# A fused mLSTM and mixture-of-experts kernel: last down products, exponent operands and ranking reordered in the steady passes

## Chip, cores and metric

One core of a Trainium2 chip. The metric is the device time of one execution in microseconds, here the median of three runs. Engines are called TensorE (PE, with its weight loads PEld), VectorE (DVE), ScalarE (ACT), GpSimd (POOL) and SyncE (SP, which issues DMAs).

## What is computed

The input `x` is 8 batches of 512 tokens with 256 features, `ctx` the same shape. The first layer adds an mLSTM attention of the normed `x` against `ctx`, with 8 heads of 32; the second adds two shared experts and the best two of eight routed experts. Cut to what matters:

```python
# attention, per batch; q = layernorm(x), k = v = ctx
cs = cumsum(log_sigmoid(fg), axis=1)                   # fg, ig: gates of [q, k, v], 8 heads x 512
log_D = where(causal, cs[:, :, None] - cs[:, None, :], -inf) + ig[:, None, :]
m = max(log_D, axis=-1, keepdims=True)
C = (q @ k.T) / sqrt(32) * exp(log_D - m)
h = C / (maximum(abs(C.sum(-1)), exp(-m)) + 1e-6) @ v  # then a layernorm with ln_scale
x = x + h
# experts on u = layernorm(x), 256 -> 1024 -> 256
h_s = sum over 2 shared experts of gelu(rmsnorm(u, g_s) @ W1_s + b1_s) @ W2_s + b2_s
scores = sigmoid(u @ centroids)                        # 8 routed experts, top 2
h_r = sum over the 2 chosen of score / scores.sum() * expert(rmsnorm(u, g_r))
out = x + u + h_s + h_r
```

## The kernel before

**Two stages.** The first stage (to about 850 us) does, for each of 8 batches, the attention, the shared experts and the routing, and scatters token rows sorted by expert to DRAM. The second stage runs the routed experts on tiles of 256 sorted tokens and adds them to the output. The change touches the first stage only.

**Tiling.** A batch has J = 4 blocks of 128 tokens. Attention is chunked: within a block the full causal product, and across blocks a state. The shared experts are cut into U = 16 units (2 experts x 8 hidden chunks of 128). One unit is six up matmuls (L1091), a GELU (L569) and a cast to the high half (L572) on ScalarE, the low half by a subtraction on VectorE (L811), and 12 down matmuls (L1074, `second`), which accumulate over all 16 units in two PSUM banks. Matrices are split in high and low halves, so that three matmuls make one product. `second` of unit k runs in unit k + LAG with LAG = 2; behind the last unit stand the two that are left. Hidden chunks sit in NHB = 3 rotating buffers.

**Order of work.** `passes` (L363) walks, on every engine alike, a list of step letters; each letter calls the part of that step that the engine has. Pass b does the shared experts and the routing of batch b, the attention ("back") of batch b + 1 and the start ("front") of batch b + 2. The lists are START (before the first batch), FIRST (pass 0), ORDER (passes 1 to 5 and 7) and ORDER_6 (pass 6). Each engine runs its own instructions in the order of the letters; between engines there are semaphores only. The letters:

- `U`: one unit. `H`: `hand_over`: ScalarE casts the normed tokens to their high half (`xhs`, L608), VectorE makes the low half (`xls`, L825). The first unit of a batch needs both.
- `S` and the digits, `T`, `V`, `W`, `X`: steps of `back`. In `S` GpSimd's weighted values (`wv`, L478, in the buffer `chunk`) are multiplied into the states (TensorE L997) and masked (VectorE L735). Each block has two steps with its number. The first: TensorE computes the decay exponents (L1012, L1014, from `exp_lhs` and `exp_rhs`) and scores (L1023); ScalarE takes exp (L546); VectorE multiplies both (L743, into `chunk`). The second: TensorE does the inter-block product (L1040, blocks 1 to 3) and P·V (L1045); VectorE gathers the numerators (L751 to L759). Scores of block j wait until the numerators of block j - 1 are gathered. `T` to `X` do the norms, the transposes (L1054) and the logits (L1062, L804).
- `F`, `G`, `R`, `C`: steps of `front` (`f`, `g` for batches 0 and 1): `F` twice, layer norm statistics (L620) and the normed `qn` (L641); `G` transposes, copies (L521) and head masks (L676); `R` gates; `C` the transposed rows (L983), their columns and exponents on VectorE (L699 to L711), exp on ScalarE (L536), and the exponent operands on VectorE (L713 to L723).
- `A`, `Q`, `B`, `D`, `E`: steps of `route`: `A` exp of the logits on ScalarE (L580) and the ranking on VectorE (L835 to L846); `Q` gates and rows (L850 to L869); `B` counts; `D`, `E` the bias product. `P` is VectorE's sum of the residual terms (L830).
- `finish`, at the end of each pass: VectorE waits until all 16 `second` are done, adds the down banks to `base` (L818), ScalarE issues the output DMA (L576).

The exponent operands are a number cut in three bf16 parts: `head16` (L713), the rest (L714), `tail16` (L715), the rest of that (L716), and the third part, copied to `exp_lhs` (L717) and `low16` (L718), from which eight instructions (L723) fill `exp_rhs` and signal `lhs_ready`. The lines that set the seam between two passes, in `second` and `finish`:

```python
pe.wait_ge(hlo_ready, U * b + k + 1)        # second: low half of chunk k
dve.wait_ge(unit_done, U * b + U)           # finish, VectorE
sc.wait_ge(fin_ready, b + 1)                # finish, ScalarE, then the output DMA
pe.wait_ge(lhs_ready, b + 1)                # back, ahead of the first exponent matmul
```

Of the kernel before, what the change touches and what calls it, by code (L numbers as in the profile page):

```python
# [12 lines left out]
P = 128  # L13
# [6 lines left out]
def xattn_moe_kernel(nc, x, ctxt, ig_w, ig_b, fg_w, fg_b, ln_scale, g_s, W1_s, b1_s, W2_s, b2_s,  # L20
# [40 lines left out]
    with whole:  # L61
# [288 lines left out]
        START = "f f f w w w f f w w f S w w w 0 w w 0 w w 1 w w 1 w 2 w 2 3 3 T T T V V V W h u X u".split()  # L350
        FIRST = "g g U U g U U g U g U U U g U U S 0 U 0 A 1 U 1 Q F 2 U F 2 B P 3 U 3 D G T E T T R V V V R W X C".split()
        ORDER = "S 0 H 0 U A 1 U F 1 U Q 2 U F 2 B U P 3 U 3 D U G T E U T U Z T U Z R V U V U V U R U W U X C U".split()
        ORDER_6 = "S 0 H 0 U A 1 U 1 U Q 2 U 2 B U P 3 U 3 D U T E U T T U V U V V U W U X U U U U".split()
# [7 lines left out]
        def passes(engine, parts):  # L361

            backs, fronts, routes = {}, {}, {}  # L363
            for b in range(-1, B):
                k, w = START.count("u") if b == 0 else 0, 0
                for step in START if b < 0 else FIRST if b == 0 else ORDER_6 if b == B - 2 else ORDER:
# [11 lines left out]
                    elif step == "H":  # L378
                        parts["hand_over"](b)
                    elif step == "P":  # L380
# [7 lines left out]
                    elif step in "FGRCfg":  # L388
# [9 lines left out]
                if b >= 0:  # L398
                    parts["finish"](b)
# [14 lines left out]
        with nc.Block() as block:  # L414
# [99 lines left out]
            def _(sc):  # L514
                def front(b):
# [7 lines left out]
                    yield  # L523
                    sc.wait_ge(gates_done, b + 1)
# [11 lines left out]
                    nc.scalar.activation(eexp[:, :], earg[:, :], ACT.Exp).then_inc(eexp_ready, 1)  # L536
                    yield
# [67 lines left out]
                def hand_over(b):  # L605
# [5 lines left out]
                            "base": lambda b: None, "finish": finish, "route": route})  # L611

            @block.vector
            def _(dve):
# [47 lines left out]
                def front(b):  # L662
# [9 lines left out]
                    if b == 0:  # L672
                        gate_weights()
                    dve.wait_ge(qcT_ready, J * b + J)
# [40 lines left out]
                    own.done(nc.vector.tensor_copy(tail16, rest[:, 0, :]))  # L715
                    own.done(stt(rest[:, 1, :], tail16, take_two[:, :], rest[:, 0, :], ALU.mult, ALU.add))  # L716
# [178 lines left out]
                def tables():  # L895
# [44 lines left out]
                    for h in range(TJ):  # L940
# [6 lines left out]
                             "base": to_add, "finish": finish, "route": route})  # L947

            @block.tensor
            def _(pe):  # L950
                mm, tr = nc.tensor.matmul, nc.tensor.transpose

                def front(b):
# [17 lines left out]
                    yield  # L971
                    pe.wait_ge(qcT_ready, J * b + J)
# [9 lines left out]
                    for j in range(J):  # L982
# [3 lines left out]
                       ends_rhs[:, :, :].rearrange("p j h -> p (j h)"), start=True, stop=True).then_inc(cols_done, 1)  # L986
                    yield
# [79 lines left out]
                def second(b, k):  # L1067

                    pe.wait_ge(hlo_ready, U * b + k + 1)
                    e, m = k // M, k % M  # L1070
# [9 lines left out]
                def unit(b, k):  # L1080
# [366 lines left out]
```

## Time and profile before

| what | value |
|---|---|
| three runs, median (lowest to highest) | 1325.37 us (1324.14 to 1329.71) |
| the profiled execution | 1325.87 us, span 1324.1 us |
| TensorE busy | 1160.5 us, 88% of the span |
| VectorE busy | 941.8 us, 71% |
| ScalarE busy | 805.9 us, 61% |
| GpSimd busy | 348.4 us, 26% |
| mean granted clock of TensorE | 0.933 |
| one GELU of a chunk (L569, 128x512) | 0.69 us |
| sum of all waits, P·V (L1045) for the decay product (L743) | 24.4 us in 13 |
| sum of all waits, second products (L1074) for the low half (L811) | 27.4 us in 7 |
| sum of all waits, ScalarE at L546 for the final sum (L818) | 46.9 us in 5 |

Busy time counts instructions at work, not waits. TensorE's matmuls are pipelined: a row's duration is from its start to its modelled end, and the next may start before it. The granted clock is TensorE's: 1.00 is 2.4 GHz, 0.50 is 1.2 GHz. In a timeline row the bracket at the end gives the idle time of that engine ahead of the row and what ended it.

### The profile page before, as it was taken

To read this page: it belongs to the slowest core of one execution; us is meant where nothing else is said; L and a number is where in the kernel's file an instruction comes from. 1 tells how busy PE (TensorE), PEld (TensorE's weight loads), DVE (VectorE), ACT (ScalarE), POOL (GpSimd) and SP (SyncE) were. 2 spreads that over 40 slices of the span, in tenths; PEclk is the share of its full clock that TensorE was granted. 3 is DMA by queue.
4 is the path that set the end of the run, shared out by engine and by line. 5 is a ranking of instruction groups with operands and counts; after the bars stand their busy time and mean duration, and the time that the engine had idled before them with its cause. 6 is when DMAs were issued, how large, how long until landed. Compare 5 with 4: busy or idle time off the path is not lost. (4 is left out here: it accounts for less than half of the span.)

```text
span 1324.1 us, 21782 instructions
## 1 busy us (share of the span) xinstructions
PE 1160.5 (88%) x7861; PEld 1016.8 (77%) x7861; DVE 941.8 (71%) x2263; ACT 805.9 (61%) x1392; POOL 348.4 (26%) x319
## 2 busy tenths in 40 slices
PE   2839984898998997997997979799999999999996
PEld 1537763677676775885875867799999999999996
DVE  6765659677686686595694545488888888888883
ACT  3315532554554564453564425399999999999994
POOL 7102132041131221221320202023333333333333
PEclk8859885999998998998998989899999999999998
DMA  5000000110010010010000103578888888888882
GB/s 184 32 17 17 16 33 32 32 64 33 19 47 33 29 37 32 33 33 32 33 17 17 41 1 113 160 228 236 232 219 219 223 234 237 236 226 221 219 223 25
DMA packets 141690, 136.16 MB, mean 103 GB/s; under 512 B 48598, under 2 KB 127584, under 8 KB 141584
## 3 DMA queue, kind: packets, MB, share of 16 engines
q1 hardware_dynamic: 122948, 111.68, 26.7%
q0 software_dynamic: 14304, 18.75, 8.5%
q10 hardware_dynamic: 4332, 4.34, 0.9%
q8 instruction: 63, 1.03, 0.3%
q14 instruction: 43, 0.35, 0.1%
HBM read 109.42 MB, written 25.33 MB: 102 GB/s over the span
## 5 line engine op out<-in xcount | busy, mean ns | idle before, releaser
L1328 DVE TENSOR_TENSOR wlo<-big,whi 128x512 fp32r<-128x512 f32 x312 | 220.1, 717 | 21.5 <-ACT whi L1281 14.3
L569 ACT ACTIVATE shared_hraw<-bank,b1s 128x512 f32<-128x512 f32 x128 | 88.0, 688 | 196.4 <-PE bank L1091 196.2
L1281 ACT CAST whi<-big 128x512 fp32r<-128x512 f32 x312 | 191.1, 615 | 5.4 <-PEq L414 5.1
L1253 PE MATMUL bank<-xhi,whi 128*128 128x256 f32 x624 | 175.7, 282 | 6.7 <-DVE xlo L1342 5.1
L1231 PE MATMUL bank<-whi,hhi 128*128 128x256 f32 x624 | 178.3, 286 | 0.0
L1231 PE MATMUL bank<-whi,hlo 128*128 128x256 f32 x624 | 174.6, 280 | 0.0
L1253 PE MATMUL bank<-xlo,whi 128*128 128x256 f32 x624 | 174.6, 280 | 0.0
L1231 PE MATMUL bank<-wlo,hhi 128*128 128x256 f32 x624 | 174.6, 280 | 0.0
L1253 PE MATMUL bank<-xhi,wlo 128*128 128x256 f32 x624 | 174.6, 280 | 0.0
L1074 PE MATMUL bank<-whs,shared_hhi 128*128 128x256 f32 x512 | 150.0, 293 | 27.4 <-DVE shared_hlo L811 27.4
L811 DVE TENSOR_TENSOR shared_hlo<-shared_hraw,shared_hhi 128x512 fp32r<-128x512 f32 x128 | 89.3, 703 | 117.1 <-ACT shared_hhi L572 115.1
L1303 ACT ACTIVATE hraw<-bank,b 128x256 f32<-128x256 f32 x312 | 147.8, 474 | 37.1 <-PE bank L1253 36.2
L487 POOL DMA_INDIRECT sorted_tokens<-rowbuf,slots x64 | 66.7, 1042 | 363.0 <-DVEq L887 346.0
L1074 PE MATMUL bank<-whs,shared_hlo 128*128 128x256 f32 x512 | 148.5, 290 | 0.0
L1074 PE MATMUL bank<-wls,shared_hhi 128*128 128x256 f32 x512 | 148.2, 289 | 0.0
L1372 DVE TENSOR_TENSOR hlo<-hraw,hhi 128x512 fp32r<-128x512 f32 x156 | 108.0, 692 | 55.3 <-ACT hhi L1308 49.7
L1406 POOL DMA_INDIRECT out_dram<-yt,token x78 | 134.9, 1730 | 29.4 <-issue 18.8
L1091 PE MATMUL bank<-xhs,whs 128*128 128x512 f32 x256 | 120.7, 471 | 13.1 <-DVE xls L825 7.7
L1074 PEld LDWEIGHTS bank<-whs,shared_hhi 128*128 128x128 f32 x512 | 100.7, 197 | 35.8 <-DVE shared_hlo L811 31.0
L1253 PEld LDWEIGHTS bank<-xhi,whi 128*128 128x128 f32 x624 | 118.8, 190 | 7.1 <-POOL xhi L1395 5.4
L1253 PEld LDWEIGHTS bank<-xlo,whi 128*128 128x128 f32 x624 | 119.0, 191 | 0.0
L1253 PEld LDWEIGHTS bank<-xhi,wlo 128*128 128x128 f32 x624 | 118.2, 189 | 0.0
(274 smaller groups left out, 2691.6 us busy)
## 6 DMA issues: line engine op xcount, KB each, us to landing
big<-in_L_ffn_W_r_dram SPq DMA_DIRECT2D x78, 1024.0 KB, 7.2
qcT<-sorted_tokens SPq DMA_DIRECT2D x39, 260.0 KB, 2.9
xb<-in_x_dram SPq DMA_DIRECT2D x8, 512.0 KB, 4.5
cb<-in_ctx_dram SPq DMA_DIRECT2D x8, 512.0 KB, 3.6
xr<-in_x_dram SPq DMA_DIRECT2D x8, 512.0 KB, 3.6
out_dram<-base ACTq DMA_DIRECT2D x8, 512.0 KB, 2.9
sorted_tokens<-chunk SPq DMA_DIRECT2D x9, 260.0 KB
out_dram<-yt,token POOLq DMA_INDIRECT x78, 4.0
```

The lines of the kernel that those rows point to most:

```text
L487: nc.gpsimd.indirect_dma_start(out=xs_dram, out_offset=bass.IndirectOffsetOnAxis(ap=slots[:, k, j:j + 1], axis=0), in_=rowbuf[:, j, :], in ...
L569: nc.scalar.activation(hraw[:, k % NHB, :], up_bank[k % 2][:, :], ACT.Gelu, bias=b1s[:, k // M, k % M:k % M + 1]).then_inc(gelu_done, 1)
L811: tt(hlo[:, k % NHB, :], hraw[:, k % NHB, :], hhi[:, k % NHB, :].bitcast(fp32), ALU.subtract).then_inc(hlo_ready, 1)
L1074: last = mm(down_bank[j // 2][:, (j % 2) * D:(j % 2 + 1) * D], h[:, k % NHB, j * P:(j + 1) * P], w[:, e, wsl], start=k == 0 and t == 0 and ...
L1091: last = mm(up_bank[k % 2][:, :], w[:, e, wsl], x_[:, c, :], start=c == 0 and t == 0, stop=c == KD - 1 and t == 2)
L1231: last = nc.tensor.matmul(y_bank[i][j * D // 512][:, (j * D) % 512:(j * D) % 512 + D], l[:, h, j * P:(j + 1) * P], w[i][:, wsl], start=m = ...
L1253: last = nc.tensor.matmul(ub[:, 0:T], w[i][:, wsl], x_[i][:, k, :], start=k == 0 and t == 0, stop=k == KD - 1 and t == 2)
L1281: nc.scalar.copy(whi[i][:, psl], raw[i][:, psl]).then_inc(t_whi, 1)
L1303: nc.scalar.activation(hraw[:, m % NHB, :], psum[m % NU][:, 0:T], ACT.Gelu, bias=b1[i][:, m:m + 1]).then_inc(t_gelu, 1)
L1328: nc.vector.tensor_tensor(wlo[i][:, psl], raw[i][:, psl], whi[i][:, psl].bitcast(fp32), ALU.subtract).then_inc(t_wlo, 1)
L1372: nc.vector.tensor_tensor(hlo[:, h - 1:h + 1, :], hraw[:, h - 1:h + 1, :], hhi[:, h - 1:h + 1, :].bitcast(fp32), ALU.subtract).then_inc(t_ ...
L1406: nc.gpsimd.indirect_dma_start(out=out_r, out_offset=bass.IndirectOffsetOnAxis(ap=token[n % NG][:, j:j + 1], axis=0), in_=yt[i][:, j, :], ...
```

## The change

The lists get four new letters. `L` calls a new part `late(b - 1)`: on TensorE it is the `second` of the last unit of the batch before, which no longer runs at the end of its pass; elsewhere it is empty. `Y` calls `finish(b - 1)`, which no longer runs at the end of a pass. `M` and `c` split steps of `front`: on VectorE the head masks go from `G` to `M`, and the exponent operands from L716 on go from `C` to `c`; on the other engines the new steps are empty. In ORDER and ORDER_6, `L`, `H`, `Y` stand between the two steps of block 0, so the last `second` comes behind the first scores of the next batch; `A` (ranking) goes behind the first step of block 1, `F` (statistics) behind its second; and `c` stands behind the last `U`. In START, FIRST and between `G` and `M` the new letters stand side by side with the old ones, so that the order of the instructions there stays, apart from the last `second` and `finish`. TensorE's first `second` of a batch now waits for the final sum of the batch before.

```diff
-        START = "f f f w w w f f w w f S w w w 0 w w 0 w w 1 w w 1 w 2 w 2 3 3 T T T V V V W h u X u".split()
-        FIRST = "g g U U g U U g U g U U U g U U S 0 U 0 A 1 U 1 Q F 2 U F 2 B P 3 U 3 D G T E T T R V V V R W X C".split()
-        ORDER = "S 0 H 0 U A 1 U F 1 U Q 2 U F 2 B U P 3 U 3 D U G T E U T U Z T U Z R V U V U V U R U W U X C U".split()
-        ORDER_6 = "S 0 H 0 U A 1 U 1 U Q 2 U 2 B U P 3 U 3 D U T E U T T U V U V V U W U X U U U U".split()
+        START = "f f f f w w w f f w w f f S w w w 0 w w 0 w w 1 w w 1 w 2 w 2 3 3 T T T V V V W h u X u".split()
+        FIRST = "g g U U g g U U g U g U U U g g U U S 0 U 0 A 1 U 1 Q F 2 U F 2 B P 3 U 3 D G M T E T T R V V V R W X C c".split()
+        ORDER = "S 0 L H Y 0 U 1 A U 1 F U Q 2 U F 2 B U P 3 U 3 D U G M T E U T U Z T U Z R V U V U V U R U W U X C U c".split()
+        ORDER_6 = "S 0 L H Y 0 U 1 A U 1 U Q 2 U 2 B U P 3 U 3 D U T E U T T U V U V V U W U X U U U U".split()
...
+                    elif step == "L":
+                        parts["late"](b - 1)
+                    elif step == "Y":
+                        parts["finish"](b - 1)
...
-                if b >= 0:
-                    parts["finish"](b)
+            parts["late"](B - 1)
+            parts["finish"](B - 1)
...
                     own.done(nc.vector.tensor_copy(tail16, rest[:, 0, :]))
+                    yield
                     own.done(stt(rest[:, 1, :], tail16, take_two[:, :], rest[:, 0, :], ALU.mult, ALU.add))
...
                 def second(b, k):
 
                     pe.wait_ge(hlo_ready, U * b + k + 1)
+                    if b > 0 and k == 0:
+                        pe.wait_ge(fin_ready, b)
...
                     if k == U - 1:
-                        for late in range(U - LAG, U):
-                            second(b, late)
+                        second(b, U - 2)
+
+                def late(b):
+                    second(b, U - 1)
```

The other hunks add a `yield` for each new step of `front` on the three engines that have it, and an empty `late` on ScalarE and VectorE.

## Rows read from the trace of the kernel before

**Rows 1.** The page, section 2: granted clock of TensorE in 40 slices

```profile
PEclk8859885999998998998998989899999999999998
```

**Rows 2.** By passes: stretch, length, busy (count) per engine, clock, DMA share, GB/s

```profile
320.00:411.00 91.00, 81.73 (x494) 64.89 (x494) 66.72 (x183) 48.78 (x66) 21.38 (x19) 1.00 0.10 36
411.00:507.00 96.00, 86.23 (x495) 69.27 (x495) 67.11 (x184) 48.77 (x66) 21.40 (x19) 0.94 0.10 34
```

**Rows 3.** Timeline of TensorE around three seams: start, length, engine, line

```profile
319.97 0.39 PE L1074 MATMUL bank<-whs,shared_hhi 128*128 128x256 f32 x1 [3.32 <-DVE shared_hlo L811]
...
321.51 2.86 PE L997 MATMUL bank<-chunk,cb 128*128 128x132 f32 x24
324.21 0.38 PE L1012 MATMUL bank<-causal,identb 128*128 128x512 bf16 x1
...
328.97 2.00 PE L1045 MATMUL bank<-vaug,chunk 128*128 128x99 f32 x16 [1.47 <-DVE chunk L743]
...
332.22 0.39 PE L1012 MATMUL bank<-causal,identb 128*128 128x512 bf16 x1
...
334.92 0.80 PE L1091 MATMUL bank<-xhs,whs 128*128 128x512 f32 x1
...
339.56 2.03 PE L1045 MATMUL bank<-vaug,chunk 128*128 128x99 f32 x16 [2.25 <-DVE chunk L743]
...
411.25 0.58 PE L1074 MATMUL bank<-whs,shared_hhi 128*128 128x256 f32 x1 [4.83 <-DVE shared_hlo L811]
...
698.30 0.58 PE L1074 MATMUL bank<-whs,shared_hhi 128*128 128x256 f32 x1 [4.82 <-DVE shared_hlo L811]
```

**Rows 4.** Timeline of VectorE at the seam at 406 us

```profile
405.21 1.00 DVE L716 SCALAR_TENSOR_TENSOR big<-big,take_two 56x512 f32<-56x512 bf16 x1
...
407.79 2.81 DVE L723 TENSOR_SCALAR big<-big,negsel 24x512 bf16<-24x512 bf16 x8
410.52 0.67 DVE L811 TENSOR_TENSOR shared_hlo<-shared_hraw,shared_hhi 128x512 fp32r<-128x512 f32 x1
414.21 1.28 DVE L818 TENSOR_TENSOR base<-base,bank 128x512 f32<-128x512 f32 x2 [3.02 <-PE bank L1074]
418.54 1.05 DVE L735 TENSOR_TENSOR state<-bank,blockmask 128x396 f32<-128x396 f32 x2 [3.05 <-PE bank L997]
...
422.87 1.21 DVE L825 TENSOR_TENSOR xls<-unT,xhs 128x1024 fp32r<-128x1024 f32 x1
425.14 0.50 DVE L759 COPY hn<-bank 128x132 f32<-128x132 f32 x2 [1.05 <-PE bank L1045]
```

**Rows 5.** Timelines of ScalarE and, last row, GpSimd at that seam

```profile
405.68 0.62 ACT L572 CAST shared_hhi<-shared_hraw 128x512 fp32r<-128x512 f32 x1
...
415.94 1.28 ACT L546 ACT_TABLE_LOAD   x1 [9.63 <-DVE base L818]
...
403.73 5.14 POOL L478 TENSOR_TENSOR chunk<-vaug,eexp 128x264 f32<-128x264 f32 x6 [25.66 <-ACT eexp L536]
```

**Rows 6.** Timelines of ScalarE, then VectorE, at the second decay product

```profile
335.19 1.06 ACT L546 ACTIVATE chunk<-bank 128x512 f32<-128x512 f32 x2
...
338.22 1.29 DVE L743 SCALAR_TENSOR_TENSOR chunk<-bank,chunk 128x512 f32<-128x512 f32 x2 [0.21 <-DVE sel L846]
```

**Rows 7.** Stretches at half clock, columns as in Rows 2

```profile
311.60:315.00 3.40, 3.40 (x15) 3.11 (x15) 3.23 (x9) 2.87 (x4) 2.54 (x3) 0.50 0.00 0
410.60:417.40 6.80, 6.15 (x28) 6.16 (x29) 1.88 (x3) 1.28 (x1) 0.00 (x0) 0.50 0.14 47
434.50:437.90 3.40, 3.40 (x15) 3.12 (x15) 2.36 (x11) 0.00 (x0) 0.00 (x0) 0.50 0.00 0
```

**Rows 8.** Timeline of TensorE behind the first batch's pass

```profile
232.19 1.98 PE L1023 MATMUL bank<-big,qcT 128*128 128x512 f32 x4 [0.44 <-DVE state L735]
...
246.62 3.66 PE L1045 MATMUL bank<-vaug,chunk 128*128 128x99 f32 x16 [2.60 <-DVE chunk L743]
```

**Rows 9.** Timeline of TensorE at the start of the last batch's units

```profile
796.73 0.80 PE L1091 MATMUL bank<-xhs,whs 128*128 128x512 f32 x1 [4.13 <-DVE xls L825]
```

More of the change, by code:

```diff
@@ L387, in passes @@
                         parts["idle"]()
-                    elif step in "FGRCfg":
+                    elif step in "FGMRCcfg":
                         f = 0 if step == "f" else 1 if step == "g" else b + 2
@@ L536, in front @@
                     nc.scalar.activation(eexp[:, :], earg[:, :], ACT.Exp).then_inc(eexp_ready, 1)
+                    yield
                     yield
@@ L610, in _ @@
                 passes(sc, {"front": front, "back": back, "unit": unit, "hand_over": hand_over, "split": split, "idle": lambda: None,
-                            "base": lambda b: None, "finish": finish, "route": route})
+                            "base": lambda b: None, "finish": finish, "late": lambda b: None, "route": route})
             @block.vector
@@ L673, in front @@
                         gate_weights()
+                    yield
                     dve.wait_ge(qcT_ready, J * b + J)
@@ L715, in front @@
                     own.done(nc.vector.tensor_copy(tail16, rest[:, 0, :]))
+                    yield
                     own.done(stt(rest[:, 1, :], tail16, take_two[:, :], rest[:, 0, :], ALU.mult, ALU.add))
@@ L946, in _ @@
                 passes(dve, {"front": front, "back": back, "unit": unit, "hand_over": hand_over, "split": split, "idle": lambda: None,
-                             "base": to_add, "finish": finish, "route": route})
+                             "base": to_add, "finish": finish, "late": lambda b: None, "route": route})
             @block.tensor
@@ L971, in front @@
                     yield
+                    yield
                     pe.wait_ge(qcT_ready, J * b + J)
@@ L986, in front @@
                        ends_rhs[:, :, :].rearrange("p j h -> p (j h)"), start=True, stop=True).then_inc(cols_done, 1)
+                    yield
                     yield
@@ L1141, in _ @@
                 passes(pe, {"split": lambda n: None, "idle": idle, "front": front, "back": back, "unit": unit, "hand_over": lambda b: None,
-                            "base": lambda b: None, "finish": lambda b: None, "route": route})
+                            "base": lambda b: None, "finish": lambda b: None, "late": late, "route": route})
         stage_a.close()
```

## The prediction

> **What bounds the kernel now.** I read the page first: TensorE is busy 88% of 1324.1 us, and its granted clock falls below full speed several times in the first two thirds [rows 1]. The table by passes [rows 2] says where: the attention stage ends near 850 us, and in it a steady pass (one batch's shared experts beside the next batch's attention) lasts about 91 us at clock 1.00 or nearly 96 us at 0.94. VectorE is busy 67 us of either, so it isn't full, and TensorE is never busy all of it. The expert stage behind 850 us is not touched, and I carry it over unchanged.
>
> The timeline of TensorE at the seam between two passes shows why [rows 3]. The second products of the two chunks before the last end at 411.25 - 4.83 = 406.42; TensorE then stands idle for 4.83 us until VectorE has made the low half of the last hidden chunk, runs that chunk's 12 matmuls, then the state products, then the first scores, and waits again, 1.47 us, for the first decay product. [Rows 4] give VectorE's order there: the whole preparation of the exponent operands (L699 to L723) comes ahead of that low half (L811), which starts only at 410.52, though its input from ScalarE was there at 406.30 [rows 5]. The third stall is 2.25 us before the second P·V product at 339.56 [rows 3, 6], where the second decay product stands behind the ranking. A fourth, 0.8 us in the middle of the pass, stays. So a steady pass has 4.83 + 1.47 + 2.25 = 8.55 us of stalls that the change can reach.
>
> On top comes the clock. The pass that begins at 319.97 and ends at 411.25 (91.28 us) runs at 2.4 GHz throughout; the three that follow, 411.25 to 698.30, take 95.68 us each [rows 3], and hold two stretches at half speed (1.2 GHz): 6.8 us that begin in the 4.83 us stall, and 3.4 us right behind the 2.25 us stall [rows 7]. So 10.2 us at half speed cost 4.4 us, 0.43 us per us.
>
> **The change at the seam, step by step.** I rebuild the seam at 406 us with the durations of [rows 3 to 5].
> VectorE: the first part of the operands ends with L715 at 405.2, where L716 now begins. The last low half comes next, but its input is ready only at 406.30: 1.1 us of new idle, then 0.67 us, so 407.0. The second part (L716 to L723, now 405.21 to 410.60, 5.4 us) then ends at 412.4, which is 1.8 us later than now. This is the price of the split.
> GpSimd: its six weighted products run from 403.73 to 408.87 as now.
> TensorE: the second-to-last chunk's products end at 406.4 as now. The state products follow at once; the first half of them runs to about 407.8, the other half waits for GpSimd until 408.9 and ends at 410.3: 1.1 us idle. The first scores need the exponent operands: 2.1 us idle until 412.45. Scores issue for 2.70 us (332.22 to 334.92), to 415.15. The moved 12 matmuls take 1.54 us (319.97 to 321.51), to 416.7. Their low half has been ready since 407.0.
> The first decay product: the score result comes 3.29 us behind the first exponent matmul (324.21 to 328.97 - 1.47), at 415.75; VectorE takes 1.29 us, done 417.05. State masking (1.05 us, L735) runs from 412.4 and is ready before the scores want it. ScalarE's decay no longer stands behind the output DMA of the last batch; its table load, now at 415.94 behind a 9.63 us wait, runs at about 406.4.
> The first P·V product starts at 417.15. Now, at full clock, it starts 9.00 us behind the last chunk's first matmul (319.97 to 328.97), so 411.25 + 9.00 = 420.25. **Gain 3.1 us** at full clock.
>
> **The finish step.** VectorE's final sum (1.28 us) and ScalarE's output DMA (0.38 us issue) move behind the hand-over of the next batch's input. VectorE: decay product to 417.05, hand-over 1.21, sum 1.28, so 419.55, then the first numerator copy (0.50) to 420.1. The next scores on TensorE wait for that copy and come up behind P·V and the first up products, 3.25 us (328.97 to 332.22) on, at 420.4: met, by 0.3 us. The new wait on TensorE (first second product of a batch waits for that sum) comes up near 429.6, 10 us after it is met; scores 2 are queued behind it. ScalarE's DMA issue waits for the sum until 419.55 with the first GELU queued behind it. The GELU table load (1.28 us), which now follows the cast of the hand-over in an idle stretch, starts at 419.95 instead and ends at 421.2; the up products it serves are done at 420.6, so GELU is 0.6 us late. I charge that below. The output DMA has 30 us until the base buffer is written again. SyncE's loads wait for the same events as before.
>
> **The ranking.** [Rows 6]: the decay is ready at 336.25, VectorE ranks until 338.01 and the product starts at 338.22. With the order turned, the product follows the decay. Chain from the first P·V at 417.15: up products done 420.6, GELU 421.2 to 421.9, cast 0.62, exp table 1.28, two decays 1.06, so 424.9 to 425.0; product 1.29, P·V 2 at 426.35. That is 9.2 us behind the first, against 10.59 now (328.97 to 339.56). **Gain 1.4 us**; the 0.6 us of the table load is in it. The ranking (2.7 us) lands behind the product and runs from 426.3 to 429.0, then the low half (0.69) and the second numerator (0.95, done 430.65); scores 2 come up at about 431.2, so 0.5 us to spare. The batch-norm statistics of the batch after next (1.8 us) come behind that; the third decay product is ready 0.2 us before its P·V. I cost these moves at nothing, under that thin cover; if it goes, each costs its lateness, up to 0.5 us a pass.
> The table load at 415.94 takes 1.28 us [rows 5], and where ScalarE is never short of work the activation follows it at once, so I count a switch at 1.28 us. The Trainium skill (ScalarE: Activation LUTs, "What ACT_TABLE_LOAD costs") adds a drain of about 1.38 us to each switch; by it the two switches of that chain would put the second P·V 2.8 us later, and five passes would give an estimated 14 us back. The measured rows decide.
>
> **Seams that differ.** First to second batch: the 12 matmuls (1.5 us) leave the chain to the fourth P·V of the first pass, which the later VectorE chain follows; they land in the 1.47 us stall. The masking no longer stands behind the final sum (0.44 us), and the second P·V's wait falls from 2.60 us to about 0.8 (1.8 us) [rows 8]: 3.7 us. Last batch: no scores there; ScalarE's cast and VectorE's hand-over stood behind the final sum, and the 4.13 us wait goes [rows 9]. The five seams between batches 1 to 6 give 4.5 us each, 22.5. Idle time and issue order: 3.7 + 22.5 + 4.1 = **30.3 us**.
>
> **The clock.** From 246 to 800 us the clock is low for 51 us, the VectorE-bound end of the seventh pass left out: 10.2 in each of four passes and 3.4 three times [rows 1, 7]. At 0.43 that cost 22 us. What will be low afterwards no row shows. Ends: nothing (as in the pass from 319.97, whose seam stall of 3.32 us drew no fall [rows 2, 3]), or 4.4 us a pass as in the three later ones. More than that is a rival below. The new stalls are 1.1, 2.1, 0.4, 0.9 and 0.8 us, each shorter than those before falls, but the 2.1 is near the 2.25 that preceded one. I take one stretch of 3.4 us per pass, costing 1.7, by the pass before 319.97, which had one [rows 7]: 8.5 us in five passes. Returned: 22 - 8.5 = 13.5 us.
> The Trainium skill (TensorE: Matmul & The Clock Gate, table of terms) prices time at the lower level at half of it, because of the halved rate; by that the 51 us would have cost an estimated 25.5 us, 3 more than the rows give, part of it having lain over stalls.
>
> Sum: 30.3 + 13.5 = 43.8 us. The profiled execution took 1325.87 us (span 1324.1 plus 1.8 around it), 0.5 above the median of three; 1325.87 - 43.8 = 1282.1. I say **1282**. About 0.5% (6.6 us) is what a measurement of this kernel can tell from no change.
>
> **Rivals.**
> (a) The forecast: seams as worked out, about one low stretch a pass: 1275 to 1290. Chance 0.50.
> (b) The clock falls as often as now, since the pass still has five short stalls, two of them within 4 us of each other around the state products: only the 30.3 us remain, 1295.5. Against it: the 4.83 us stall is gone. 0.18.
> (c) The clock never falls in steady passes: 1325.9 - 52.3 = 1273.6, down to 1270 with small extra. For it: stalls of 3.32 and 1.47 us passed without a fall at 316 to 329. 0.14.
> (d) The second P·V gives back. VectorE or ScalarE is late after the first one: sum ahead of the numerator copy, GELU behind the output DMA, ranking ahead of the second numerator. If the 1.4 us goes and the clock is as in (b): 30.3 - 7 = 23 us, 1303. 0.11.
> (e) **Slower.** The place is the seam: the exponent operands are ready 1.8 us later and the state products are split by a wait, so low-intensity work lies from 406.4 to 412.4. If the clock falls there and stays low through scores and P·V, each slower chunk makes the next stall. The change loses once a pass has more than 10.2 + 4.5/0.43, about 21 us, at half speed (seams one and seven apart); with 27 us it costs 11.6 a pass, 2.7 more than the 8.9 at stake, so 13.5 less 7.8 from the end seams: 1331 to 1332. For it: from 411 on every pass had both falls. Against: none had more than 10.2. 0.04.
> (f) It does not do what it says: the first scores turn out bound by what feeds the operands, all waits shift by 1.8 us and the time stays within 6.6 us. 0.03.
>
> **How the numbers follow.** Faster by over 0.5%: (a) to (d), 0.93; same 0.03, slower 0.04. The range 1270 to 1304 takes in (a) to (d) with their ends and leaves out (e), (f) and the tails.
>
> **What would show it.** The low half of the last chunk directly behind L715, with about 1.1 us wait for ScalarE; on TensorE, before the states a wait of 1.1 us for GpSimd and before the first scores about 2.1 us for VectorE's L723 line (new numbers), instead of 4.83 for the low half; second products between scores and first P·V; the wait before P·V down from 1.47 to 0.4 and from 2.25 to 0.9; ScalarE's wait for the final sum (9.6 us) replaced by one of some 3 us; steady passes 87 to 89 us long; no 4.13 us wait at the last batch. I am wrong if passes stay above 91 us, if the granted clock in steady passes stays at 0.94, or if a stall over 3 us stands anywhere in the new seam.

## The result, and the profile after

The changed kernel takes **1274.43 us** (median of four, 1273.78 to 1274.91) against 1325.36 for the kernel before in the same series (four, 1324.14 to 1329.71). The ratio is 0.961, with a 95% interval of 0.9588 to 0.9632. So it is 51 us faster, where 43.8 us (1282) were forecast.

The page of the changed kernel, its first lines and the granted clock in 40 slices:

```profile
span 1271.8 us, 21794 instructions
...
PE 1141.1 (90%) x7861; PEld 996.1 (78%) x7861; DVE 936.4 (74%) x2263; ACT 806.3 (63%) x1392; POOL 349.3 (27%) x319
...
PEclk9858986999999999999999999899999999999998
```

Three steady passes of the changed kernel, then the two stretches at half speed that are left in the steady passes (columns as in [rows 2]):

```profile
230.00:316.00 86.00, 81.79 (x495) 64.99 (x494) 66.02 (x183) 48.78 (x66) 21.43 (x19) 1.00 0.12 42
316.00:402.00 86.00, 81.81 (x495) 64.98 (x494) 65.97 (x183) 48.78 (x66) 21.30 (x19) 1.00 0.11 36
402.00:490.00 88.00, 83.85 (x496) 65.84 (x495) 66.03 (x184) 48.79 (x66) 21.42 (x19) 0.98 0.11 39
...
402.80:406.20 3.40, 3.40 (x7) 1.57 (x6) 0.34 (x1) 1.73 (x3) 0.00 (x0) 0.50 0.03 8
576.90:580.30 3.40, 3.40 (x10) 1.86 (x9) 0.91 (x2) 1.43 (x3) 0.00 (x0) 0.50 0.00 0
```

Set beside [rows 2]: the same work of every engine, in 86 us instead of 91 at clock 1.00, and in 88 instead of 96 where the clock fell. TensorE's busy time in a full-clock pass is the same (81.8 us), so what went is idle time.

TensorE of the changed kernel at one seam (the answer to [rows 3]; the moved second products, L1086, run from 317.68 to 319.67, between the scores and P·V), and two up products of the last batch: its first (the answer to [rows 9]) and the first of its fourth unit:

```profile
309.35 1.51 PE L1007 MATMUL bank<-chunk,cb 128*128 128x132 f32 x12
312.06 1.62 PE L1007 MATMUL bank<-chunk,cb 128*128 128x132 f32 x12 [1.20 <-POOL chunk L482]
314.98 0.39 PE L1022 MATMUL bank<-causal,identb 128*128 128x512 bf16 x1 [1.30 <-DVE big L731]
...
316.26 1.98 PE L1033 MATMUL bank<-big,qcT 128*128 128x512 f32 x4
317.68 0.69 PE L1086 MATMUL bank<-whs,shared_hhi 128*128 128x256 f32 x1
...
319.72 2.00 PE L1055 MATMUL bank<-vaug,chunk 128*128 128x99 f32 x16
...
328.82 2.03 PE L1055 MATMUL bank<-vaug,chunk 128*128 128x99 f32 x16 [0.67 <-DVE chunk L751]
...
745.17 0.40 PE L1103 MATMUL bank<-xhs,whs 128*128 128x512 f32 x1
...
752.05 0.50 PE L1103 MATMUL bank<-xhs,whs 128*128 128x512 f32 x1 [1.10 <-ACT shared_hraw L575]
```

That fourth unit in the kernel before:

```profile
804.63 0.50 PE L1091 MATMUL bank<-xhs,whs 128*128 128x512 f32 x1 [0.67 <-ACT shared_hraw L569]
```

The 4.83 us stall is gone, and so is the 1.47 us before P·V. In their place stand 1.20 us for GpSimd and 1.30 us for the exponent operands. The 2.25 us before the second P·V are 0.67. The 4.13 us of the last batch are gone: its first up product follows the products ahead of it at once. The wait for a GELU three units later grew from 0.67 to 1.10 us.

VectorE of the changed kernel at that seam (the answer to [rows 4]): the low half L819 (L811 before) stands ahead of the second part of the operands, the hand-over L833 ahead of the final sum L826 (L818 before), the second decay product L751 ahead of the ranking L843:

```profile
309.49 0.99 DVE L819 TENSOR_TENSOR shared_hlo<-shared_hraw,shared_hhi 128x512 fp32r<-128x512 f32 x1 [1.22 <-ACT shared_hhi L578]
310.41 1.11 DVE L724 SCALAR_TENSOR_TENSOR big<-big,take_two 56x512 f32<-56x512 bf16 x1
311.55 0.73 DVE L725 CAST exp_lhs<-big 24x512 bf16<-24x512 f32 x1
312.30 0.41 DVE L726 CAST big<-big 24x512 bf16<-24x512 f32 x1
312.75 2.18 DVE L731 TENSOR_SCALAR big<-big,negsel 24x512 bf16<-24x512 bf16 x8
314.85 1.03 DVE L743 TENSOR_TENSOR state<-bank,blockmask 128x396 f32<-128x396 f32 x2
318.28 1.29 DVE L751 SCALAR_TENSOR_TENSOR chunk<-bank,chunk 128x512 f32<-128x512 f32 x2 [2.40 <-PE bank L1033]
319.49 1.22 DVE L833 TENSOR_TENSOR xls<-unT,xhs 128x1024 fp32r<-128x1024 f32 x1
320.62 1.28 DVE L826 TENSOR_TENSOR base<-base,bank 128x512 f32<-128x512 f32 x2
321.82 0.49 DVE L767 COPY hn<-bank 128x132 f32<-128x132 f32 x2
...
327.47 1.29 DVE L751 SCALAR_TENSOR_TENSOR chunk<-bank,chunk 128x512 f32<-128x512 f32 x2 [1.77 <-ACT chunk L552]
328.68 0.17 DVE L843 TENSOR_SCALAR prob<-prob 128x32 f32<-128x32 f32 x1
```

ScalarE of the changed kernel there (the answer to [rows 5, 6]); the wait of 9.63 us is 3.95, and what waits is now the table load of GELU, behind the output DMA:

```profile
309.41 1.28 ACT L552 ACT_TABLE_LOAD   x1
...
322.34 1.28 ACT L575 ACT_TABLE_LOAD   x1 [3.95 <-DVE base L826]
...
326.29 1.09 ACT L552 ACTIVATE chunk<-bank 128x512 f32<-128x512 f32 x2
```

**Where the 51 us come from.** I measure passes from one second P·V product to the next, six of them in the steady stretch: 246.62 to 720.62 us before, which is 474.0, and 242.63 to 676.11 after, which is 433.5. That is 40.5 us for five passes. A pass at full clock went from 91.28 to 86.19 us, 5.1 shorter, which makes 25.5; the other 15 is time at half speed. The 246.62 that became 242.63 are 4.0 us. The second P·V of the pass before it shows that 0.9 of them were there ahead of the first seam, so the seam itself gave 3.1. Before, then after:

```profile
161.67 1.92 PE L1045 MATMUL bank<-vaug,chunk 128*128 128x99 f32 x16
...
160.81 1.92 PE L1055 MATMUL bank<-vaug,chunk 128*128 128x99 f32 x16
```

Between the last P·V of the six and the first product of the second stage lie 135.5 us before (to 856.1) and 127.4 after (to 803.49): 8.1 us. The last batch's waits give 3.7 of it (4.13 to nothing, 0.67 to 1.10). The other 4.4 go with the clock, which was low for 17 us before and for 3.4 after (a stretch of 10.2 us at the edge of the second stage, in both kernels, left out): stretches of 3.4 us at 721.2 and 796.3, which have no counterpart after, cost about 3.1, and the one of 10.2 us at 765.6, of which 3.4 are left at 723.7, cost 1.2 more. Spans of the two profiled executions differ by 52.3 us (1324.1 and 1271.8), the medians by 50.9.

### The profile page after: what moved, and what is told of

Same layout as the page of the kernel before. It is cut to its first block and busy times, and to the rows that moved or that the text cites. A ratio compares the mean times of both kernels' runs of the same rounds, so it can differ in the third digit from the quotient of the medians.

```text
span 1271.8 us, 21794 instructions
## 1 busy us (share of the span) xinstructions
PE 1141.1 (90%) x7861; PEld 996.1 (78%) x7861; DVE 936.4 (74%) x2263; ACT 806.3 (63%) x1392; POOL 349.3 (27%) x319
## 5 line engine op out<-in xcount | busy, mean ns | idle before, releaser
L819 DVE TENSOR_TENSOR shared_hlo<-shared_hraw,shared_hhi 128x512 fp32r<-128x512 f32 x128 | 90.9, 716 | 106.1 <-ACT shared_hhi L578 103.1
L1086 PE MATMUL bank<-whs,shared_hhi 128*128 128x256 f32 x512 | 149.0, 291 | 4.8 <-DVE shared_hlo L819 4.8
L1086 PE MATMUL bank<-whs,shared_hlo 128*128 128x256 f32 x512 | 145.1, 283 | 0.0
L1086 PE MATMUL bank<-wls,shared_hhi 128*128 128x256 f32 x512 | 144.8, 283 | 0.0
L1103 PE MATMUL bank<-xhs,whs 128*128 128x512 f32 x256 | 117.5, 459 | 9.5 <-ACT shared_hraw L575 5.9
L1245 PEld LDWEIGHTS bank<-whi,hhi 128*128 128x128 f32 x624 | 117.7, 189 | 0.0
```

Of the source, the lines that this page charges most:

```text
L819: tt(hlo[:, k % NHB, :], hraw[:, k % NHB, :], hhi[:, k % NHB, :].bitcast(fp32), ALU.subtract).then_inc(hlo_ready, 1)
L1086: last = mm(down_bank[j // 2][:, (j % 2) * D:(j % 2 + 1) * D], h[:, k % NHB, j * P:(j + 1) * P], w[:, e, wsl], start=k == 0 and t == 0 and ...
L1103: last = mm(up_bank[k % 2][:, :], w[:, e, wsl], x_[:, c, :], start=c == 0 and t == 0, stop=c == KD - 1 and t == 2)
L1245: last = nc.tensor.matmul(y_bank[i][j * D // 512][:, (j * D) % 512:(j * D) % 512 + D], l[:, h, j * P:(j + 1) * P], w[i][:, wsl], start=m = ...
```

## The experiments

In all of them the kernel before was run in the same series; its medians were 1329.5, 1328.3, 1330.4 and 1330.6 us in the four series, so kernels of different series are compared by their ratios. All ratios are to the kernel before. The changed kernel itself, run again in the second series ("control"), took 1274.6 us (1274.44 to 1276.79), ratio 0.960 (0.9575 to 0.9626). The third series (unsplit_2, split_only, tuned) ran on another chip than the first, second and fourth, and only the second has a run of the changed kernel itself.

> The changed kernel itself again, beside the others. In the profiles of the four runs so far ScalarE starts one copy per pass (L591, the transposed gates) 1.0 us or more late and the GELU behind it 2.4 us late, with no engine as releaser, and TensorE then waits 1.2 us for a low half; neither profile of the first comparison had that. If it belongs to the chip or its state and not to the order of the program, it stands in this profile too, and the time is 1278 to 1281. If it belongs to the order of the edited programs, this profile is as the first one and the time 1274 to 1275.

**1. The clock alone: the kernel before, with more work.** Matmuls whose results nobody reads are put into two of the stalls; no computation is left out.

```diff
                     if k == U - 1:
-                        for late in range(U - LAG, U):
-                            second(b, late)
+                        second(b, U - 2)
+                        if 0 < b < B - 2:
+                            pe.wait_ge(gelu_done, U * b + U)
+                            for _ in range(6):
+                                fill(5)
+                        second(b, U - 1)
...
+                        if b > 1 and j == 1:
+                            pe.wait_ge(gelu_done, U * (b - 1) + 1)
+                            for _ in range(3):
+                                fill(4)
                         pe.wait_ge(ct_ready, J * b + j + 1)
```

> The kernel before with TensorE's two stalls of each steady pass filled by matmuls that nobody reads: six of 128x512 in the 4.83 us stall, three in the 2.25 us stall (from the pass of batch 1 on). Nothing else moves. Theory (low clock costs time of its own): the half-speed stretches behind these stalls go, and the steady passes take about 91.3 us instead of 95.7: 18 to 22 us less than the kernel before. Rival (the stalls are the whole cost and the low clock is hidden in waits): no change, or up to 5 us more where the filling is late.

Measured: 1310.26 us (1308.68 to 1311.63), ratio 0.9866 (0.9834 to 0.9897). Two passes of this kernel, by second P·V, and one pass of the kernel before:

```profile
246.70:338.40 91.70, 89.23 (x514) 68.29 (x514) 67.24 (x185) 48.78 (x66) 21.41 (x19) 1.00 0.10 35
338.40:431.30 92.90, 90.46 (x513) 69.34 (x512) 66.86 (x184) 48.79 (x66) 21.42 (x19) 0.98 0.11 35
```

```profile
433.70:529.40 95.70, 86.18 (x495) 69.19 (x495) 66.96 (x184) 48.77 (x66) 21.40 (x19) 0.95 0.10 34
```

With 18 more matmul instructions a pass (513 for 495) and every chain on the other engines as before, passes are 91.4 to 93.0 us instead of 95.6. Only two stretches of 3.4 us at half speed are left in the steady passes. So some 18 us of the kernel before (16 between the two profiled executions) were the clock's alone, and they can be had without moving anything. That is the lower end of what was expected.

**2. The parts, alone and undone.** Each of the three parts alone, on the kernel before. The ranking and statistics moved ("rank_only"):

```diff
-        ORDER = "S 0 H 0 U A 1 U F 1 U Q 2 ...
+        ORDER = "S 0 H 0 U 1 A U 1 F U Q 2 ...
```

> The kernel before with the ranking and the statistics behind the second decay product and the numerators, and nothing else. Theory: 1.5 us a pass in six passes, and no half-speed stretch behind the second P.V (up to 1.65 us in four or five passes): 9 to 17 us less than the kernel before. Rival (the later falls of the clock only move to another place): 7 to 9 us less.

The operands split ("split_only": `C` ends at L715, and `c` with the rest stands behind the last `U`):

```diff
-        ORDER = "... W U X C U".split()
+        ORDER = "... W U X C U c".split()
...
                     own.done(nc.vector.tensor_copy(tail16, rest[:, 0, :]))
+                    yield
```

> The kernel before with the exponent operands in two parts and nothing else: the second part behind the last low half. Theory: the 4.83 us stall falls to 0.7, but the final sum now queues behind the second part on VectorE and delays masking and decay, so the first P.V comes 2 to 2.5 us earlier; the 6.8 us at half speed go, the 3.4 us behind the second P.V stay: 20 to 26 us less than the kernel before. Rival (only issue order matters, the clock falls as often): 10 to 13 us less.

And the changed kernel without split and without the new place of the ranking, which leaves the late second product and the late final sum ("late_only"):

```diff
-        ORDER = "S 0 L H Y 0 U 1 A U 1 F U Q 2 ... W U X C U c".split()
+        ORDER = "S 0 L H Y 0 U A 1 U F 1 U Q 2 ... W U X C c U".split()
```

> The kernel before with one part of the change alone: last second products and final sum behind the next batch's first scores; operands in one part, ranking ahead of the decay. Theory: it is rank_first with the unsplit operands, so a seam about 1 us shorter: 3 to 5 us under rank_first, 1296 to 1299. Rival (the parts need each other, the low half behind the operands still holds up the products): over 1305.

| kernel | us (lowest to highest) | ratio (95%) | steady pass | gain |
|---|---|---|---|---|
| rank_only | 1308.8 (1308.61 to 1309.79) | 0.9854 (0.9823 to 0.9884) | 92.2 | 19.5 |
| split_only | 1296.84 (1292.96 to 1299.23) | 0.9765 (0.9736 to 0.9793) | 88.6 | 33.6 |
| late_only | 1290.38 (1288.67 to 1292.04) | 0.9715 (0.9684 to 0.9747) | 88.8 | 37.9 |
| all (control) | 1274.6 (1274.44 to 1276.79) | 0.960 (0.9575 to 0.9626) | 86.2, two of 87.5 and 87.8 | 53.7 |

The three gains add up to 91 us, and together they give 53.7. They overlap, because moving the last product and splitting the operands remove one and the same 4.83 us stall, and because the same time at half speed is given back by more than one of them. A later steady pass of the kernel before has 10.2 us of it, one of rank_only 6.8, of late_only 3.4, of split_only none. All three parts gained more than was expected of them: 9 to 17 us for rank_only, 20 to 26 for split_only (a fall of the clock was expected behind its 2.25 us stall, and did not come), and 1296 to 1299 us for late_only. TensorE of split_only at one seam, with all its waits; the 4.83 are 1.03 already:

```profile
491.30 0.38 PE L1077 MATMUL bank<-whs,shared_hhi 128*128 128x256 f32 x1 [1.03 <-DVE shared_hlo L813]
...
497.89 1.99 PE L1026 MATMUL bank<-big,qcT 128*128 128x512 f32 x4 [0.80 <-DVE state L737]
...
501.35 2.00 PE L1048 MATMUL bank<-vaug,chunk 128*128 128x99 f32 x16 [1.47 <-DVE chunk L745]
...
511.96 2.03 PE L1048 MATMUL bank<-vaug,chunk 128*128 128x99 f32 x16 [2.25 <-DVE chunk L745]
```

The half-speed stretch of rank_only at the seam: its 4.83 us stall stays, and so do 6.8 us at half speed in each pass, as in [rows 7], while the second stretch is gone with the 2.25 us stall:

```profile
408.00:414.80 6.80, 6.13 (x28) 6.13 (x29) 1.90 (x4) 1.28 (x1) 0.00 (x0) 0.50 0.13 46
```

In late_only it is the other way round. Its stall before the second P·V grew to 2.53 us, and 3.4 us at half speed follow it in every pass:

```profile
422.51 2.89 PE L1055 MATMUL bank<-vaug,chunk 128*128 128x99 f32 x15 [2.53 <-DVE chunk L751]
```

```profile
423.20:426.60 3.40, 3.40 (x15) 3.21 (x15) 2.39 (x11) 0.00 (x0) 0.00 (x0) 0.51 0.00 0
```

Two kernels undo one part of the changed kernel. "rank_first" puts `A` and `F` back to where they stood. "seam_old" puts the last second product and the final sum back to the end of the pass, and keeps split and ranking:

```diff
rank_first
-        ORDER = "S 0 L H Y 0 U 1 A U 1 F U Q 2 ...
+        ORDER = "S 0 L H Y 0 U A 1 U F 1 U Q 2 ...
seam_old
-        ORDER = "S 0 L H Y 0 U 1 A U ...
+        ORDER = "S 0 H 0 U 1 A U ...
...
-            parts["late"](B - 1)
-            parts["finish"](B - 1)
+                if b >= 0:
+                    parts["finish"](b)
...
                         second(b, U - 2)
+                        second(b, U - 1)
```

> The changed kernel with ranking and statistics ahead of the decay product and the numerators again (U A 1 U F 1). Theory: the second P.V waits 2.2 us instead of 0.67 in each of six passes (9 us), and the clock falls again behind part of these stalls, up to 1.65 us each: 1283 to 1292. Rival (ranking order only shifts work along VectorE): 1274 to 1277. Clock rival: the falls came from the 4.83 us stall alone, then no half-speed stretch follows the 2.2 us stalls and the time is at most 1284.

> The changed kernel with the last second products and the final sum at the end of their own pass again; split and ranking stay. Theory: the split alone takes most of the 4.83 us stall (0.6 left), and the moved products and sum are worth about 0.7 us a pass plus 4.1 at the last batch and 2 at the first seam: about 1284. Rival (the move of the products carries the seam): all of the 3.6 us a pass comes back, 1298 or more.

Measured: rank_first 1301.85 us (1301.02 to 1303.09), ratio 0.9793 (0.9731 to 0.9855); seam_old 1286.71 (1283.45 to 1290.45), 0.9676 (0.9612 to 0.974). Both came from the first series, which had a disturbance that part 3 describes, so seam_old was run once more. The old place of the ranking costs nearly 2% of the time in that series, a stall of 2.53 us in each pass and more stretches at half speed; rank_first is 10 us slower than the slowest that was expected. (The series has no run of the changed kernel; unsplit and split_later of part 3, which have the new place, are at 0.9596 and 0.9613.) The cleanest pair are late_only and unsplit_2 of part 3, which differ in nothing but this place: 88.8 against 85.2 us a pass, ratios 0.9715 and 0.9534, though in two series.

> The kernel of seam_old once more, since its profile had ScalarE late once per pass. Split and ranking in place, last products and final sum at the end of their own pass. Theory: free of that, the steady pass is 86.3 + 0.7, about 87.0 us, with next to no half-speed time, and the whole 1281 to 1284: the move of the products is worth 7 to 9 us beside the split. Rival (the lateness of ScalarE cost nothing here): 88.0 us a pass and 1286 as before.

Measured: 1280.71 us (1276.85 to 1282.33), ratio 0.964 (0.9615 to 0.9664), passes of 86.6 us with one of 87.8. Once operands and ranking are in their new places, moving the second product and the final sum brings 0.4 us a pass. On the whole time it is about 5 us (0.964 against 0.960, intervals that just overlap), less than the 7 to 9 expected. From the last second P·V to the second stage seam_old_2 takes 134.0 us (676.68 to 810.66), the control 127.2 (679.28 to 806.52). So the most part of what this move adds lies behind the steady passes, where the wait of 4.13 us at the last batch stays without it and 17 us instead of 3.4 run at half speed (the edge of the second stage again left out).

**3. Is the split needed?** "unsplit" is the changed kernel with `c` directly behind `C`; "split_later" splits one instruction later, behind L724.

```diff
unsplit
-        ORDER = "... W U X C U c".split()
+        ORDER = "... W U X C c U".split()
split_later
-                    yield
                     own.done(stt(rest[:, 1, :], tail16, take_two[:, :], rest[:, 0, :], ALU.mult, ALU.add))
+                    yield
```

> The changed kernel with the exponent operands in one part again (c ahead of the last U in ORDER). Theory: with the last second products behind the first scores, the low half of the last chunk is no longer urgent, so the split only delays the operands: in the trace of the changed kernel VectorE idles 1.22 us for ScalarE and the scores wait 1.30 us for L731. Unsplit, the operands are ready about 1.2 us earlier, the masking of the states then follows the low half and takes back some 0.4: 0.9 us a pass, 4 to 5 us, 1269.5 to 1270.5. Rival (the split earns part of the 51 us): slower than 1274.4 by 3 to 15 us.

> The changed kernel with the cut of the exponent operands one instruction later (L724 of its page, about 1.0 us, runs before the last low half instead of behind it). Theory: it fills the 1.22 us in which VectorE waits for ScalarE, so the operands are ready 1.0 us earlier and the 1.30 us wait falls to about 0.3: 5 us in five passes, about 1269.5. Rival (GpSimd's weighted products bound the seam, or VectorE slows down beside GpSimd by as much): within 1 us of 1274.4.

Measured: unsplit 1275.26 us (1272.6 to 1278.98), ratio 0.9596 (0.9549 to 0.9644); split_later 1278.26 (1273.16 to 1279.98), 0.9613 (0.9565 to 0.9661). Neither told anything, because of something in this series that I did not expect. Once in each pass ScalarE was late: a copy that follows a matmul began 1 us later, and the GELU behind it waited for something on no engine. ScalarE of unsplit, and behind it the wait of TensorE that came of it:

```profile
270.71 0.57 ACT L591 COPY frow<-bank 8x512 f32<-8x512 f32 x1 [3.74 <-PE bank L1130]
...
273.54 0.69 ACT L575 ACTIVATE shared_hraw<-bank,b1s 128x512 f32<-128x512 f32 x1 [2.26 <-remote]
...
297.94 0.38 PE L1086 MATMUL bank<-whs,shared_hhi 128*128 128x256 f32 x1 [1.23 <-DVE shared_hlo L819]
```

ScalarE of control at the same place:

```profile
270.46 0.58 ACT L591 COPY frow<-bank 8x512 f32<-8x512 f32 x1 [2.74 <-PE bank L1130]
...
271.87 0.69 ACT L575 ACTIVATE shared_hraw<-bank,b1s 128x512 f32<-128x512 f32 x1 [0.83 <-PE bank L1103]
```

All four profiles of the first series had it, and none of any later series, the same programs among them. So it goes with the series and not with the edits. I ran unsplit again, beside kernels without the lateness.

> The kernel of unsplit once more. Its profile had ScalarE late by 2.4 us once per pass, as the three others of that series, and the repeated changed kernel in the next series had not. If that came from the chip or its state, this profile is free of it, the steady passes take 85.2 us (86.19 less 0.97 of the shorter seam) and the time is 1269 to 1271. If it belongs to the program, the passes take 86.6 us again and the time is 1275.

Measured: **1267.86 us** (1263.59 to 1268.72), ratio 0.9534 (0.951 to 0.9558), which is below the changed kernel's interval, and a little below the 1269 to 1271 expected. The two were never in one series, so this rests on the ratios and on the passes. Every steady pass takes 85.23 us, and none has time at half speed. TensorE of unsplit_2 at a seam:

```profile
398.70 1.62 PE L1007 MATMUL bank<-chunk,cb 128*128 128x132 f32 x12 [1.00 <-POOL chunk L482]
400.43 0.39 PE L1022 MATMUL bank<-causal,identb 128*128 128x512 bf16 x1
...
401.98 1.98 PE L1033 MATMUL bank<-big,qcT 128*128 128x512 f32 x4 [0.20 <-DVE state L743]
```

VectorE of unsplit_2 there:

```profile
397.56 2.81 DVE L731 TENSOR_SCALAR big<-big,negsel 24x512 bf16<-24x512 bf16 x8
400.30 0.67 DVE L819 TENSOR_TENSOR shared_hlo<-shared_hraw,shared_hhi 128x512 fp32r<-128x512 f32 x1
400.90 1.03 DVE L743 TENSOR_TENSOR state<-bank,blockmask 128x396 f32<-128x396 f32 x2
```

The operands are ready at 400.37, the moment at which the state products are through, so the exponent products wait for nothing and the scores 0.20 us for the masking. With the split, VectorE stands idle 1.22 us for the low half's input, and the operands come 1.3 us too late. The low half itself has no hurry any more, since its products run behind the scores. The split thus costs 1.0 us a pass (86.19 against 85.23). The two half-speed stretches of the changed kernel begin not quite 2 us behind the 1.30 us stall that it leaves; that this stall brings them is not shown, since three passes with the same stall have none.

**4. A version that beats both.** From unsplit, the low half of the last chunk is put behind the state masking (letter `K`), by a part that VectorE alone has, and SyncE issues the output DMAs of batches 0 to 5, so that no GELU stands behind them on ScalarE:

```diff
-        ORDER = "S 0 L H Y 0 U 1 A ...
+        ORDER = "S K 0 L H Y 0 U 1 A ...
...
+                def out_dma(b):
+                    sp.wait_ge(fin_ready, b + 1)
+                    sp.dma_start(out_v[b], base[:, :, :]).then_inc(s_base_out, 16)
...
                 def finish(b):
+                    if b < B - 2:
+                        return
```

> The changed kernel with operands unsplit, VectorE's low half of the last chunk behind the masking of the states (0.2 us of wait less), and the output DMAs of batches 0 to 5 issued by SyncE, so that ScalarE's GELU table load no longer follows the final sum (the 0.67 us wait of the second P.V should fall to about 0.1). Theory: 0.97 + 0.2 + 0.55 us a pass, 84.5 us per steady pass, 1264 to 1267. Rival (GpSimd's weighted products and the second P.V's own chain bound the pass): as unsplit_2.

Measured: **1263.17 us** (1260.64 to 1266.89), ratio 0.9508 (0.9484 to 0.9532), in the same series as unsplit_2, 4.7 us below it, though the two intervals of the ratio overlap; against the changed kernel's they don't. Passes of 84.5 us. TensorE of tuned before its second P·V, where the changed kernel waits 0.67 us:

```profile
410.88 2.03 PE L1074 MATMUL bank<-vaug,chunk 128*128 128x99 f32 x16 [0.28 <-DVE chunk L763]
```

The two edits were not run apart; of the 0.7 us a pass the rows give 0.4 at the second P·V (0.67 to 0.28, where 0.1 was expected) and 0.2 at the scores. What is left of waits in its steady pass is that, 0.80 us for a GELU, and in three of five passes 1.0 us for GpSimd's weighted values.

The other two passes have a stretch at half speed ahead of the seam instead. A pass of tuned with such a stretch, one with none, then the stretch; the other such stretch, at 474.3, is alike, in a pass of 84.5 us too:

```profile
326.40:410.90 84.50, 83.17 (x495) 66.28 (x495) 66.69 (x184) 48.82 (x67) 21.39 (x19) 0.98 0.11 38
495.40:579.90 84.50, 82.10 (x495) 65.22 (x495) 66.64 (x184) 48.78 (x67) 21.39 (x19) 1.00 0.12 39
...
389.00:392.40 3.40, 3.40 (x12) 2.82 (x12) 3.23 (x11) 2.16 (x3) 1.80 (x2) 0.50 0.00 0
```

They cost nothing. TensorE comes to the state products 1.5 us later (68.2 us into the pass instead of 66.7), its 1.0 us wait for GpSimd is gone, and the first exponent matmul starts 71.1 us into the pass either way. So TensorE and its clock don't set the length of the pass ahead of the seam, and 0.43 us per us is a price of the kernel before, not of every place.

## Why the prediction was right, and where its sizes were off

**The seam, step by step: right.** From the end of the second-to-last chunk's products to the first P·V the forecast had 10.73 us (406.42 to 417.15); measured are 10.21 (309.51 to 319.72). VectorE's new idle was put at 1.1 and is 1.22, TensorE's wait for GpSimd at 1.1 and is 1.20. TensorE's wait for the operands was put at 2.1 and is 1.30: their second part takes 4.5 us (310.41 to 314.93) and not 5.4, because the terms came from a place where VectorE ran beside GpSimd for most of it, to 408.87. Now GpSimd ends at 312.01, and behind that the same instructions are shorter (L726 0.41 us against 0.75, the eight of L731 2.18 against 2.81, where two ran beside GpSimd). On the other side the low half, now beside GpSimd, takes 0.99 us and not 0.67. The state products end 0.3 us later than put (313.68), which takes the rest of the difference off the wait.
The wait of 0.4 us before the first P·V is not there. The decay product came out as put, ready 4.59 us behind the first exponent matmul (forecast 4.60). But from the moved products' first matmul to P·V it is 2.04 us (317.68 to 319.72) and not 1.54, so TensorE is still at work when the decay product is ready. One step has no row in the profile of before and came out as written: the low half does not hold TensorE up, since it is ready 7 us before its products.

**Finish step and ranking: right.** The first numerator copy ends 2.6 us behind the first P·V (forecast 2.95), so the next scores find it done. The GELU table load ends 3.9 us behind it (forecast 4.05). First to second P·V: forecast 9.2 us, measured 9.10. The row of the load, 1.28 us and the activation at its end, held: a further 2.8 us, which the drain named by the Trainium skill (ScalarE: Activation LUTs, "What ACT_TABLE_LOAD costs") would have put there, are not there.
The ranking, the low half and the numerators behind the second decay product delay nothing; no wait over 0.2 us stands on TensorE between 328.8 and the 0.80 us stall near 379. Undone, they cost the stall again (2.53 us in late_only).

**Ends: right, both a little too much.** I put 3.7 us at the first seam, and 3.1 are measured. The 4.13 us of the last batch are wholly gone as forecast; 0.4 us come back three units later, where the wait for a GELU grew, which the forecast did not have.

**The clock: mis-sized.** This is the step "I take one stretch of 3.4 us per pass, costing 1.7: 8.5 us in five passes". Measured: two such stretches in five passes, which cost 1.4 and 1.1 us (passes of 87.58 and 87.33 against 86.19). That is 2.5 us, so 6.0 of the 8.5 were charged too much. The 22 us that the clock was said to cost before come out at 20.7 (474.0 less five passes of 91.28, and 3.1 behind them), so 18.2 us are returned where 13.5 were forecast.

The five seams add 3.0 (passes shortened by 5.1 us instead of 4.5, which makes them 86.2 us long at full clock, 87.3 and 87.6 with a fall, where 87 to 89 were forecast), the first seam takes off 0.6 and the last batch 0.4.

With these the forecast's 43.8 becomes 50.5. The 52.3 between the spans leave 1.8: 0.9 that was there ahead of the first seam, 1.2 from the stretch at 765.6, which the forecast had left out, less 0.3 in the second stage. The two large errors, 4.7 and 3.0 us, went the same way, so no luck of errors that cancel made the number.

The result lies between my case (a), 1275 to 1290, and case (c), a clock that never falls, 1270 to 1273.6, and I had the weight between them too far towards (a). That returned clock time is real is what "filled" shows: 18 us without any shorter chain. Nor is two stretches a property of the program: the control, the same kernel, has three in these passes, at 405.8, 655.0 and 665.2.

**Rivals.** (b), as many falls as before, is excluded by the windows. (d), the second P·V gives back, by its 9.10 us. (e), slower through a clock that stays low at the seam: the clock does fall there, over the first scores and the moved products (402.8 to 406.2), but for 3.4 us in two passes of five, where more than 21 us in each would have been needed. (f), nothing moves, by the ratio.

**What the forecast did not ask.** It priced the change as a whole, and not whether its parts cost each other. It called the split's 1.8 us of later operands a price, and took the split as needed for the whole. Once the last product is moved, it isn't: without it the kernel is faster.

## What to carry to other kernels

When two edits aim at one stall, price the second again with the first one in place: here the move alone or the split alone takes away the 4.83 us, and both together wait 1.3 us for what the split makes late. Take the time that the granted clock costs as a sum of its own, read from passes at either level, and expect most of it back once the longest stall of a pass is gone (6.8 of 10.2 us in late_only, all in split_only). Ask too whether TensorE has a wait behind the slow stretch, since in tuned such stretches cost nothing. Take an instruction's duration from a place with the same neighbours, since VectorE instructions of these sizes took about 0.3 us longer each where they ran beside GpSimd.

## What the runs showed of the chip beyond that

A stall's length alone does not tell whether the clock falls. In the kernel before, stalls of 2.25 us were followed by half speed in four passes, from 433.7 on [rows 7], but not the one at 339.56, nor the 3.32 us that ended at 319.97 [rows 3]. The 2.25 us stall of split_only (the last row of its fence) drew none in its steady passes, from 423 to 689 us, and 2.53 us in late_only drew one each time. What lay ahead in the pass differs between them, and which of it decides stays open. The Trainium skill (TensorE: Matmul & The Clock Gate, "Why this matters for your kernels") warns of gaps over about 3 us between bursts of matmuls. The runs here don't agree with that as a boundary: falls came behind stalls of 2.53 and 2.25 us, and none behind 3.32 us.

The lateness of ScalarE in the first series, 2.4 us once a pass with no engine as its releaser, cost TensorE about 1.2 us a pass. It was in the profiles of all four kernels of that series and in no later profile, and its cause stays open. A comparison that is to settle 1 us a pass needs both kernels in a series without it.
